# The last attention of each batch one period later in a hand-ordered, five-engine pipeline

## What is computed

```python
h = _self_attn(_ln(x) * (1 + sc_msa) + sh_msa, ...);        x = x + h * g_msa
h = _topk_cross_attn(_ln(x) * (1 + sc_mca) + sh_mca, ...);  x = x + h * g_mca
h = _swiglu(_ln(x) * (1 + sc_mlp) + sh_mlp, ...);           x = x + h * g_mlp
q = _ada_ln(x, ...) @ Wq;  kv = _ada_ln(ctx, ...) @ Wkv
x = x + softmax(q k^T / sqrt(16)) v @ Wp + bp
```

## Time and profile before

| | us |
|---|---|
| Median of 3 runs | 1279.81 |
| Lowest and highest run | 1276.47 to 1280.52 |
| The profiled execution, its own time | 1284.55 |
| Its span, first to last instruction | 1282.4 |

### The profile page before, as it was taken

The page is one execution under the profiler, slowest core; times in us unless marked ns, Lnnn a source line. Parts: engine busy times, 40 slices in busy tenths (PEclk is TensorE's granted clock), DMA queues, the critical chain, the costliest instruction groups (busy, mean ns, idle before and its releaser), DMA issues. The chain is left out here.

```text
span 1282.4 us, 39016 instructions
## 1 busy us (share of the span) xinstructions
PE 1200.6 (94%) x13666; PEld 853.9 (67%) x13666; DVE 1128.0 (88%) x3812; ACT 1034.6 (81%) x2193; POOL 855.0 (67%) x1134
## 2 busy tenths in 40 slices
PE   6778899999999999999999999999999999989987
PEld 6665566667676776767676766767676776656654
DVE  3579999899999999999999989999999999997443
ACT  3745688889898979889797979889797979786764
POOL 1415597959587877859686877959596867776210
PEclk8988999999999999999999999999999999999989
DMA  7542021202121121212021212212121111111111
GB/s 200 149 92 56 22 60 35 63 25 57 39 56 44 47 64 52 57 34 69 21 68 35 64 47 54 58 31 57 28 59 42 47 48 35 43 26 27 26 26 34
DMA packets 111391, 67.25 MB, mean 52 GB/s; under 512 B 13836, under 2 KB 107870, under 8 KB 111198
## 3 DMA queue, kind: packets, MB, share of 16 engines
q1 hardware_dynamic: 109166, 63.71, 19.0%
q10 hardware_dynamic: 2032, 1.05, 0.5%
HBM read 22.33 MB, written 4.19 MB: 21 GB/s over the span
## 5 line engine op out<-in xcount | busy, mean ns | idle before, releaser
L1246 ACT ACTIVATE prob<-turned_score 128x1024 f32<-128x1024 f32 x320 | 325.8, 1018 | 78.5 <-PE turned_score L908 76.1
L1521 POOL TENSOR_TENSOR pair<-full,pair 128x512 f16<-128x512 f32 x182 | 210.9, 1162 | 118.2 <-ACT pair L1201 113.6
L1405 DVE MATCH_REPLACE8 rest<-top,score 128x256 f32<-128x256 f32 x512 | 208.9, 417 | 0.0
L1419 DVE MATCH_REPLACE8 far<-best,rest 128x256 bf16<-128x256 f32 x512 | 206.4, 412 | 0.0
L1402 DVE MAX8 top<-score 128x8 f32<-128x256 f32 x512 | 193.9, 421 | 13.2 <-PE score L908 12.4
L1527 POOL TENSOR_SCALAR far<-far 128x512 bf16<-128x512 bf16 x256 | 158.6, 620 | 41.4 <-DVE far L1419 20.9
L1392 DVE TENSOR_REDUCE rowmax_l<-score 128x4 f32<-128x1024 f32 x121 | 147.8, 1221 | 30.4 <-PE score L908 24.3
L908 PE MATMUL work<-pair_n,w_m_hi 128*128 128x256 f16 x1024 | 173.5, 273 | 0.3 <-ACT full L1194 0.2
L908 PE MATMUL work<-pair_n,w_m_lo 128*128 128x256 f16 x512 | 139.6, 273 | 0.0
L1201 ACT ACTIVATE pair<-full 128x512 f16<-128x512 f32 x192 | 121.1, 631 | 20.2 <-DMA k_stack_l<-pair 1.8
L908 PEld LDWEIGHTS work<-pair_n,w_m_hi 128*128 128x128 f16 x1024 | 96.1, 98 | 19.1 <-issue 7.6
(11 more groups left out here) (212 smaller groups left out, 3206.8 us busy)
## 6 DMA issues: line engine op xcount, KB each, us to landing
k_stack_t<-pair SPq DMA_DIRECT2D x96, 64.0 KB, 2.5
k_stack_l<-pair SPq DMA_DIRECT2D x96, 64.0 KB, 2.6
q_stack_w<-pair SPq DMA_DIRECT2D x93, 64.0 KB, 2.6
k_stack_w<-pair SPq DMA_DIRECT2D x93, 64.0 KB, 2.6
q_stack_t<-pair SPq DMA_DIRECT2D x93, 64.0 KB, 2.6
q_stack_l<-pair SPq DMA_DIRECT2D x93, 64.0 KB, 2.6
ctx_t<-in_ctx_turned SPq DMA_DIRECT2D x16, 256.0 KB, 2.9
ctx_l<-in_ctx SPq DMA_DIRECT2D x16, 256.0 KB, 3.1
```

Of the source, the lines that this page charges most:

```text
L1246: act.activation(prob[:, at:at + 2, :], both_b[:, :, :], ACT.Exp).then_inc(exp_done, 1)
L1405: m = dve.match_replace(rest[p % 2][:, t, :], eight[:, t, :], bank[:, t * L:(t + 1) * L], -FAR)
L1419: m = dve.match_replace(far[p % NFAR][:, t, :], best[p % 2][:, t, :], rest[p % 2][:, t, :], -FAR)
L1521: pool.tensor_tensor(pr[:, 1, :, :], whole[:, :, :], pr[:, 0, :, :], ALU.subtract).then_inc(split_lo, 1)
```

## The change

The entries of the five lists are the same before and after: 1639 on TensorE, 1235 on ScalarE, 889 on VectorE, 733 on GpSimd, 373 on SyncE. Only their order differs, the filler matmuls, and one wait.

- All work of step l (and of n4 and the second context) of batch b stands about one period later, beside w of batch b+5 instead of b+4. The first `a_l:0` stands after `a_w:4` instead of after `a_w:3`. From `a_w:3` to `a_w:4` TensorE's list has 73 entries and none of l, where it had 91 with 16 of l; from `a_w:4` to `a_w:5` it has 88 with 15 of l, where it had 101 with 31. In the later periods it has 101 to 103 in both.
- From `a_w:15` to `m1:15` the list has 193 entries instead of 205, and from `m1:15` to its end 110 instead of 78. Those 110 hold 24 of `a_l` and 25 of `b_l` (batches 13, 14, 15), where there were 16 and 17 (14 and 15). After `m2:15:3` come 20 entries of `a_l` instead of 12. `x4_n4:15`, with which the last batch's l begins, stands 37 entries behind `m2:15:3` instead of 9; from it to `a_l:15` there are 19 entries instead of 11, and from `a_l:15` to the end 31 instead of 35.
- On SyncE the store `xo:0` stands directly ahead of `gg_w:6`, and `pr_l:0`, whose result it waits for, is 3 entries ahead of `gd_w:6` on TensorE. Before, 35 entries lay between `pr_l:0` and the newest TensorE entry that SyncE had already served. It is alike for several later batches.
- `ms` of n2, n3 and n4 waits for the `rs` of the batch before, on its own engine.
- There are 504 filler matmuls instead of 474. Ahead of `m1:15` there are 382 (366 before), after it 122 (108).

The core of the diff; the other lists are rearranged in the same way:

```diff
...
-        "vj_w:3 x4_n2:2 o_t:1 pj_tk:2 a_t:1:6 gd_t:1:2 m1:0:4 b_t:1:2 m1:0:5 b_t:1:3 pj_tq:2 a_w:3 m1:0:6 a_t:1:7 "
...
-        "a_l:0:5 o_t:2:1 gd_l:0:1 a_t:2:7 b_l:0:1 m1:1:6 m1:1:7 b_t:2:4 a_w:4 o_l:0 b_t:2:5 a_w:4:1 gd_t:2:3 "
-        "gd_w:4 gd_l:0:2 o_t:2:2 a_w:4:2 m2:1 gd_w:4:1 a_t:3 b_t:2:6 m2:1:1 b_t:2:7 m2:1:2 a_l:0:6 b_l:0:2 m2:1:3 "
...
-        "m1:2:7 o_l:1 a_w:5 b_t:3:5 gd_l:1:1 gd_t:3:3 pr_l:0 a_w:5:1 o_t:3:2 b_t:3:6 a_w:5:2 gd_w:5 m2:2 gd_w:5:1 "
...
-        "pj_lq:14 a_l:13:6 b_l:13:4 a_l:13:7 b_l:13:5 o_l:13:1 gd_l:13:3 x4_n3:15 o_l:13:2 b_l:13:6 m1:15 m1:15:1 "
-        "m1:15:2 a_l:14 b_l:13:7 m1:15:3 vj_l:14 a_l:14:1 o_l:13:3 m1:15:4 m1:15:5 a_l:14:2 gd_l:14 ot_l:13 "
-        "m1:15:6 m1:15:7 b_l:14 a_l:14:3 bk_l:13 x4_nc:15 m2:15 m2:15:1 m2:15:2 m2:15:3 gd_l:14:1 b_l:14:1 "
-        "xt_m:15 pr_l:13 a_l:14:4 b_l:14:2 pj_lk:15 a_l:14:5 x4_n4:15 o_l:14 b_l:14:3 pj_lq:15 a_l:14:6 gd_l:14:2 "
-        "vj_l:15 a_l:14:7 b_l:14:4 o_l:14:1 gd_l:14:3 a_l:15 b_l:14:5 a_l:15:1 b_l:14:6 o_l:14:2 a_l:15:2 gd_l:15 "
-        "b_l:14:7 a_l:15:3 o_l:14:3 b_l:15 a_l:15:4 gd_l:15:1 ot_l:14 a_l:15:5 b_l:15:1 bk_l:14 b_l:15:2 a_l:15:6 "
-        "gd_l:15:2 a_l:15:7 b_l:15:3 o_l:15 b_l:15:4 gd_l:15:3 pr_l:14 b_l:15:5 o_l:15:1 b_l:15:6 o_l:15:2 "
-        "b_l:15:7 o_l:15:3 ot_l:15 bk_l:15 pr_l:15"),
...
+        "b_t:1:2 vj_w:3 x4_n2:2 pj_tk:2 o_t:1 a_t:1:6 gd_t:1:2 m1:0:4 m1:0:5 b_t:1:3 a_w:3 pj_tq:2 m1:0:6 a_t:1:7 "
...
+        "a_t:2:7 pj_tq:3 m1:1:6 a_w:4 x4_nc:0 m1:1:7 b_t:2:4 a_w:4:1 o_t:2:1 gd_w:4 gd_t:2:3 m2:1 a_w:4:2 b_t:2:5 "
+        "m2:1:1 a_t:3 b_t:2:6 gd_w:4:1 gd_w:4:2 o_t:2:2 m2:1:2 a_w:4:3 b_t:2:7 m2:1:3 o_t:2:3 b_w:4 xt_m:1 ot_t:2 "
...
+        "o_t:3:1 m1:2:5 a_l:0:4 pj_tq:4 a_l:0:5 m1:2:6 a_t:3:7 b_l:0:1 m1:2:7 b_t:3:4 a_w:5 gd_l:0:1 gd_t:3:3 "
...
+        "m2:12:2 a_w:15 b_t:13:7 a_w:15:1 gd_w:15 m2:12:3 a_w:15:2 o_t:13:3 b_w:15 gd_w:15:1 a_w:15:3 xt_m:12 "
...
+        "o_l:12:1 b_l:12:5 x4_n3:15 o_l:12:2 b_l:12:6 m1:15 m1:15:1 m1:15:2 b_l:12:7 a_l:13 m1:15:3 o_l:12:3 "
+        "a_l:13:1 vj_l:13 m1:15:4 m1:15:5 a_l:13:2 gd_l:13 ot_l:12 m1:15:6 m1:15:7 x4_nc:14 b_l:13 a_l:13:3 "
+        "bk_l:12 m2:15 m2:15:1 m2:15:2 m2:15:3 pj_lk:14 a_l:13:4 x4_n4:14 gd_l:13:1 a_l:13:5 b_l:13:1 a_l:13:6 "
+        "xt_m:15 gd_l:13:2 pj_lq:14 o_l:13 a_l:13:7 b_l:13:2 b_l:13:3 pr_l:12 b_l:13:4 gd_l:13:3 vj_l:14 o_l:13:1 "
+        "b_l:13:5 x4_nc:15 a_l:14 b_l:13:6 a_l:14:1 o_l:13:2 a_l:14:2 gd_l:14 b_l:13:7 a_l:14:3 o_l:13:3 b_l:14 "
+        "a_l:14:4 gd_l:14:1 ot_l:13 b_l:14:1 pj_lk:15 x4_n4:15 b_l:14:2 bk_l:13 a_l:14:5 gd_l:14:2 o_l:14 "
+        "a_l:14:6 b_l:14:3 pj_lq:15 a_l:14:7 b_l:14:4 pr_l:13 gd_l:14:3 b_l:14:5 o_l:14:1 vj_l:15 b_l:14:6 "
+        "o_l:14:2 b_l:14:7 a_l:15 o_l:14:3 a_l:15:1 ot_l:14 a_l:15:2 gd_l:15 bk_l:14 a_l:15:3 b_l:15 a_l:15:4 "
+        "gd_l:15:1 b_l:15:1 a_l:15:5 pr_l:14 a_l:15:6 gd_l:15:2 b_l:15:2 o_l:15 a_l:15:7 b_l:15:3 gd_l:15:3 "
+        "b_l:15:4 o_l:15:1 b_l:15:5 b_l:15:6 o_l:15:2 b_l:15:7 o_l:15:3 ot_l:15 bk_l:15 pr_l:15"),
...
-        "gg_w:5:1 gg_l:1:2 gg_w:5:2 gg_w:5:3 xi:7 gg_t:4 xo:0 in_lq:2 in_lk:2 gg_l:1:3 gg_t:4:1 in_wq:6 in_tk:5 "
...
-        "gg_l:2:3 gg_t:5 in_lk:3 xi:8 in_lq:3 gg_t:5:1 in_tk:6 gg_l:3 in_wq:7 gg_t:5:2 xo:1 cl:5 in_wk:7 in_tq:6 "
...
+        "in_lq:1 xi:7 gg_t:4:1 in_wq:6 in_tk:5 gg_l:1 cl:3 in_wk:6 gg_t:4:2 in_tq:5 gg_t:4:3 xo:0 gg_w:6 gg_l:1:1 "
...
+        "cl:4 in_tk:6 in_wk:7 gg_t:5:2 gg_l:2:1 ct:7 in_tq:6 gg_t:5:3 xo:1 gg_w:7 gg_w:7:1 gg_w:7:2 xi:9 gg_l:2:2 "
...
 
 
-IDLE_WORK = ("pj_wq:0:0=59 gd_w:0:0=30 gd_w:0:1=21 gd_w:0:2=11 bk_w:0:0=17 x4_n2:0:0=25 pj_tq:0:0=38 a_w:1:0=13 "
-             "a_t:0:0=16 a_w:1:2=35 o_w:1:0=14 gd_t:0:1=27 b_t:0:3=7 gd_t:0:2=9 o_t:0:2=11 a_t:1:0=11 pr_w:2:0=12 "
-             "a_l:13:7=10 ot_l:13:0=8 xt_m:15:0=6 x4_n4:15:0=5 a_l:15:1=15 a_l:15:3=11 a_l:15:7=16 bk_l:15:0=14 "
-             "pr_l:15:0=33")
+IDLE_WORK = ("pj_wq:0:0=70 a_w:0:0=21 gd_w:0:1=21 gd_w:0:2=11 bk_w:0:0=17 xt_w:0:0=16 x4_n2:0:0=25 wp:0:17=8 "
+             "a_w:1:0=33 a_t:0:0=20 b_w:1:0=38 a_w:1:3=20 a_t:0:1=30 pr_w:1:0=6 a_t:0:5=6 o_t:0:0=6 a_t:1:0=5 "
+             "bk_t:0:0=6 a_t:1:3=23 a_l:13:5=9 a_l:13:6=15 a_l:14:1=9 a_l:14:3=11 gd_l:14:2=18 b_l:15:0=6 "
+             "a_l:15:5=7 bk_l:15:0=14 pr_l:15:0=33")
 
 
 def idle_work():
@@ -1487,6 +1487,8 @@
                 kind, _, s = piece.partition("_")
                 if kind == "ms":
                     pool.wait_ge(x_added[ADDED[s]], b + 1)
+                    if b > 0:
+                        pool.wait_ge(norm_done[s], b)
                     pool.tensor_scalar(rstd[s][:, 2, :], row_sum[s][:, :], -1.0 / C, 0.0, ALU.mult,
                                        ALU.add).then_inc(mean_done[s], 1)
                 elif kind == "rs":

```

## The result

The changed kernel takes 1302.74 us (median of 4 runs, 1301.32 to 1304.27), the kernel before in the same session 1278.14 us (1275.87 to 1280.52). The ratio is 1.0185, 95% interval 1.0164 to 1.0205. The forecast was 1280.0, with a range up to 1289.

What follows compares the result with a forecast made beforehand. TensorE was taken to pace the middle, VectorE the period without l. -14.3 + 14 = -0.3 us, applied to the median of 1279.81 with half a microsecond for fillers, gave 1280.0 us; own range 1276 to 1284, of all 1270 to 1289.

Steps and rivals of the forecast that it cites:

- The fill: Period from `a_w:3` without l, bounded by VectorE: 57.3 us instead of 71.6, so -14.3 us (bounds -16.0 and -9.8).
- The start: First periods, up to `a_w:3`: given no term of their own in the forecast's sum.
- The middle: Periods from `a_w:5` to `a_w:15`, same content with l of another batch: 0, with 5 us on both sides.
- The last t: Stretch from `a_w:15` to `m1:15`, 76 entries of l instead of 80: 0, inside the same 5 us.
- The new wait, fillers, stores: `ms` wait on GpSimd, 30 more fillers, SyncE's stores: 0 each; uncovered under 2 us, 2.4 us, 2 us a place.
- The drain: Behind `m1:15`, three l's open instead of two: +14 us, the middle between +11.1 and +17.
- 16.8 us more of TensorE: TensorE's work on one more l in the drain: group sums 199.8 x 0.672 / 8 = 16.8 us for a batch.
- what can absorb it is the hole: TensorE's idle time ahead of `a_l:15`, 13.51 - 7.85 = 5.7 us, could take in part of the added l.
- the lower bound: Least cost of the drain: 16.8 us of added TensorE work less 5.7 us of idle time ahead of `a_l:15`, +11.1.
- The upper bound: Most for the drain: eight more l entries through the score banks at 2.08 us each, +16.6, rounded to 17.
- The faster one: VectorE is the pace throughout: -13.2 in the period without l, +8 in the drain, sum -5.2; 1274 us, chance 0.31.
- The slower one: Drain paced by the loop of score, maximum and exponential: +17, fill only 9.8; sum +7.2, 1287 us, chance 0.29.

Runs made afterwards that it cites:

- the two seams in the middle: Two kernels with the lists of before up to some 40 us into the period of `a_w:8` or `a_w:12`, the changed lists after: 1307.63 and 1311.91 us.
- the first kernel by bank: Changed kernel with the maxima of `l:13` and `l:14` taken bank by bank, as those of `l:15` are: ratio 1.0198 to the kernel before.
- old start: Changed kernel with the lists and fillers of before up to `a_w:2`, the changed ones from there: 1296.99 us, ratio 1.0153 to the kernel before.
- old start and by bank: Changed kernel with before's lists up to `a_w:2` and the maxima of `l:13` and `l:14` bank by bank: 1294.6 us, ratio 1.0117.

## Why the prediction was wrong, step by step

- **The fill, -14.3: right in kind, somewhat large.** -13.3 in this profile. In all twelve profiles with the changed lists there, `a_w:3` to `a_w:5` takes 132.2 to 133.1 us, in the six with before's 143.6 to 145.9: -11.7 in the mean. In the period from `a_w:3` VectorE is 99% busy and TensorE 90%, as forecast. The place of `a_w:5`, about 310, was missed (316.57), mostly for the start's sake; by the forecast's own sign a time past 316 spoke for slower.
- **The start, taken as unchanged: wrong by 3 us.** The forecast's sum had no term for the order of the first periods.
- **The middle, 0: right.** `a_w:5` to `a_w:14` is 643.7 for 644.0, and between 642.9 and 645.0 in all sixteen profiles without a seam in it. (TensorE's waits for exponentials, 3.3 of 10.7 us idle, were the largest part of its idle time, not most of it as said.)
- **The last t, 0: wrong by 4 to 5 us.** From `a_w:14` to `m1:15` it is +4.3 here; 234.1 to 239.1 us with the changed lists, 230.1 to 233.2 with before's. I had counted the entries behind `a_w:15` only (they took 8.0 us less) and taken the period ahead of it as one like the others. It has 11 entries more, three of them m, and 12.2 us more went by. TensorE's work over both is no larger (219.8 busy for 221.8); its idle time grew by 6.3 us. What in the order of these lists makes it wasn't tested and stays open.
- **The new wait, fillers, stores: nothing found against them.** The wait costs nothing in the old order, and a drain without fillers isn't faster. The fillers of the start weren't run apart from its order, and no run singled out the stores; the middle as a whole didn't get longer.
- **The drain, +14: the step that failed.** +23.7 here, +24.7 in the mean, and 20 to 23 for an l left out. Of its two halves, "16.8 us more of TensorE" was too small. That weight had been scaled by 0.672, the overlap of groups in the full mix; in the drain TensorE's busy time grew by 20.9 us for one l and 14 fillers (an estimated 1.1 us at 79 ns each), at no lower a clock (0.95 for 0.93). The other half, "what can absorb it is the hole", took 5.7 us off for the lower bound and 2.8 for the middle. The hole did shrink, by 3.3 us, but the idle time around it grew by 6.1, so nothing was absorbed and 2.8 us came on top: 20.9 + 2.8 = 23.7. The upper bound was too low for the same reason. It took the loop of score to score, 2.08 us a unit, for the whole pace, while `l:14` and the way to `l:15` took 26.4 us, 3.3 a unit: products, guard rows and a load of 4.12 us lie between the units.
- **The rivals.** The faster one, with VectorE as the pace throughout, looked for the gain on the wrong side: the fill gave 11.7 in the mean where it had 13.2, and the idle VectorE of the drain took nothing off. With the two seams in the middle an l less gave VectorE idle time and not speed. The slower one named the right place, and a fill closer to the measured one (9.8), with too small a price for the drain.

With the means of what was measured, the sum is -11.7 + 3.4 + 5.4 + 24.7 = +21.8 where the forecast had -0.3. Of the 22.1 us between them the drain makes 10.7, the last t 5.4, the start 3.4 and the fill 2.6. None of the variants of the changed kernel with all their work came below the kernel before.

## What to carry to other kernels

Moving a stage one period back adds one such stage to the end. Its price there is more than it weighs inside the mix (17 us here) and less than the distance from one start to the next in the last stretch (26); measured, it was 20 to 24. The surest way to know it is to leave the last one out and take the difference. The hole at the beginning gave 12 to 13; a delay pays only if the fill is worth more than that price. Where an engine is half idle, a further microsecond on it can still arrive in full; "it has room" is an argument for throughput, not for a chain.

## What was unexpected of the hardware

The granted clock differs from one execution to the next, and so the time, where the instructions don't: four runs of the first kernel by bank took 1299.8 us at a mean clock of 0.977, 1302.3 at 0.977, 1307.4 at 0.970 and 1310.3 at 0.967. In the profiles much of it falls at the end. Behind `a_l:15`, the same 260 matmuls in the same lists took 31.1 us at 0.95 (old start), 33.1 at 0.85 (by bank), 33.5 at 0.85 (the changed kernel) and 37.6 at 0.68 (old start and by bank). That is 6 us of scatter from one stretch, more than most effects looked for in it. The stretch ahead of it scatters less, and it shows the price of the added l by itself: from `m1:15` to `a_l:15` it takes 42.8 to 43.0 us in three profiles with before's drain and 66.0 to 67.7 in seven with the changed one. The last of them:

```profile
1187.90:1253.90 66.00, 60.75 (x630) 40.88 (x630) 35.15 (x64) 51.97 (x105) 17.63 (x27) 1.00 0.16 39
1253.90:1291.50 37.60, 31.74 (x260) 17.65 (x260) 13.54 (x23) 14.36 (x24) 1.15 (x1) 0.68 0.11 29
```
